# Graph layer on one core: h transposed by DMA in place of TensorE, with attention and aggregation moved within a set

## The chip, the cores and the metric

One NeuronCore of a Trainium2 chip runs the whole program. The metric is device time in microseconds (us); the time of the kernel before is the median of three runs.

## The reference, cut to what matters

There are 128 graphs of 64 nodes with 384 features. With the drawn data every edge has some type, and type 0 means no edge; the layer is

```
h = relu(layernorm(x))                                   # 128 x 64 x 384
hi_t = h @ W1[:384] + dep_emb @ W1[384:] + b1            # per pair i, j
hj_t = h @ W2[:384] + dep_emb @ W2[384:] + b2
relevance = sum(hi_t * hj_t, -1);  A = softmax(where(adj, relevance, -1e9))
out = x + relu((A @ h) @ gcn_w + gcn_b) @ Wo + bo
```

The adjacency holds only 0 and 1 here, so the edge embedding is one vector, and relevance reduces to (h M + bias) h^T plus a row term, with M = W1 W2^T. The aggregation is done on hg = h @ gcn_w.

## The kernel before, in words

The 128 graphs are worked in 16 sets of 512 tokens (NSUP = 16; s counts them). A set is 4 tiles of 128 tokens (KT), each of 2 graphs (GT), and the 384 features are 3 chunks of 128 (DC). The matrix products are split: each float32 operand is a float16 high part and a float16 low part (what the high part leaves), and a product is three float16 matmuls, high by high, high by low and low by high (split_product, L974 to L976).

Five instruction streams, one for each engine, are written out by hand in order, with semaphores between them. A stream is in order: a waiting instruction holds all that stands behind it. In iteration s:

* **TensorE** (PE): G of set s = M^T h^T in three chunks (g_chunk); the transposes of attention of set s-1 (L1137) after the first chunk; the aggregation of set s-1 (L1184, L1189) into three z banks; four tiles of hg of set s (hg_tile); the scores of set s (L1031); 12 transposes of h of set s+1 (L1020, float32, into PSUM); four output tiles of set s-1.
* **ScalarE** (ACT): copies of G (L454), of transposed attention (L532), of z (L545) and of the high part of hg (L459); of the scores (L564); the high part of h^T out of PSUM (L450); the exponentials (L572); and at the end `normalise(s + 2)`, four activations that write h_tok (L441).
* **VectorE** (DVE): high part of G (L706), attention high (L824), high part of z (L829), statistics of set s+2 (L595), row term and low part of hg (L865, L632), masks and scores (L883 to L896), low part of h^T (L601), softmax (L917 to L929), the outputs added into x (L836).
* **GpSimd** (POOL): low part of G (L354), low part of z (L401), the 20 small steps of layer norm's coefficients of set s+2 (L318), then the output bias added to x of set s (L408).
* **SyncE** (SP) issues DMAs: load of set s+4 (L236), four SBUF to SBUF moves of hg (L250, L251), store of a finished set (L241).

So the coefficients of set s+2 need its statistics, `normalise(s + 2)` needs the coefficients, and the h^T of set s+2 is needed by G one iteration later. Ahead of the loop a startup makes M, finds the scales of the weights, and looks whether any edge type over 1 is there (`typed`, skipped here). In the startup PE multiplies hg of set 0 first and then G of set 0. Iterations 1, 14 and 15 and the tail are written out apart.

The eight PSUM banks are shared: `G_BANK = (1, 2, 0)`, `Z_BANK = (3, 4, 5)`, `HG_BANK = (1, 2, 0, 3)`, `T_BANK = (4, 5, 0)` and `O_BANK = (1, 2, 3, 4)`; bank 6 is for scores, bank 7 for attention.

Of the kernel before, what the change touches and what calls it, by code (L numbers as in the profile page):

```python
# [5 lines left out]
def gnn_layer_program(nc, x, adj, emb, W1, b1, W2, b2, gcn_w, gcn_b, Wo, bo, out):  # L6
# [50 lines left out]
    with ctx:  # L57
# [3 lines left out]
        def sem(name):  # L61
# [4 lines left out]
        w1_dep = sb("w1_dep", [DE + 1, D])  # L66
        w2_dep = sb("w2_dep", [DE + 1, D])
        e_col = sb("e_col", [DE + 1, 1])
        e_wide = sb("e_wide", [DE + 1, P])
        q_row = sb("q_row", [P, D])  # L70
        product = sb("product", [P, D])
# [3 lines left out]
        wo_raw = sb("wo_raw", [P, DC, D])  # L75
# [38 lines left out]
        m_raw = x_all[:, NSUP - 5, 0:DC, :]  # L114
        stats6 = sb("stats6", [P, KT, 6])
# [10 lines left out]
        hT_hi = sb("hT_hi", [P, DC, N], f16)  # L126
        hT_lo = sb("hT_lo", [P, DC, N], f16)
# [49 lines left out]
        ty_vec = sb("ty_vec", [P, 2, DC, NT])  # L177
        ty_pq = sb("ty_pq", [P, NT])
        ty_value = sb("ty_value", [P, NT])
        ty_row = sb("ty_row", [P, KT, NT])  # L180
# [5 lines left out]
        G_BANK, Z_BANK, HG_BANK, T_BANK, O_BANK = (1, 2, 0), (3, 4, 5), (1, 2, 0, 3), (4, 5, 0), (1, 2, 3, 4)  # L186

        LAST_Z_BANK = (5, 0, 6)
# [11 lines left out]
            top_types top_types_all types_known consts_made bias_made stats_ready coef_ready h_ready t_done  # L200
            t_high t_split g_done g_copied g_high g_split hg_done hg_high hg_split dot_done s_done scored
# [11 lines left out]
         top_types, top_types_all, types_known, consts_made, bias_made, stats_ready, coef_ready, h_ready, t_done,  # L213
         t_high, t_split, g_done, g_copied, g_high, g_split, hg_done, hg_high, hg_split, dot_done, s_done,
# [19 lines left out]
        def _(sp):  # L234
# [7 lines left out]

            def move_hg(s):
# [20 lines left out]
            for s in range(2, 4):  # L264
                sp.wait_ge(x_loaded, 16 * s)
                load_x(s)

# [10 lines left out]
            with sp.Fori(0, NSUP - 4) as s:  # L278

                sp.wait_ge(x_loaded, 16 * (s + 4))  # L280
                load_x(s + 4)
                move_hg(s + 1)
                store_out(s)
            with sp.Fori(NSUP - 4, LAST) as s:
                move_hg(s + 1)
                store_out(s)
# [8 lines left out]
        def _(pool):  # L295
# [45 lines left out]
            def main_coefficients(s):  # L341

                pool.wait_ge(stats_ready, s + 1)

                if not isinstance(s, int) or s >= 1:
                    pool.wait_ge(h_ready, KT * s)
                coefficients(s, stats6, ln_mul, ln_add, coef_ready)
# [46 lines left out]
            def iteration(s, prev=True, cur=True, nxt2=True):  # L394
# [10 lines left out]
                if cur:  # L405

                    pool.wait_ge(h_ready, KT * (s + 1))
# [14 lines left out]
        def _(act):  # L422
# [21 lines left out]
            def transposed_high(s):  # L444

                if not isinstance(s, int) or s >= 1:
                    act.wait_ge(s_done, s)
                for c in range(DC):
                    act.wait_ge(t_done, DC * s + c + 1)
                    nc.scalar.activation(hT_hi[:, c, :], bank[T_BANK[c]][:, :], ACT.Copy).then_inc(t_high, 1)  # L450
# [40 lines left out]
            transposed_high(0)  # L491
# [28 lines left out]
            def iteration(s, prev=True, prev2=True, cur=True, nxt=True, nxt2=True):  # L520
                z_bank = Z_BANK if cur else LAST_Z_BANK
                for c in range(DC):
# [4 lines left out]
                    if c == (0 if prev2 else DC - 1) and prev:  # L527
# [39 lines left out]
                if nxt:  # L567
                    transposed_high(s + 1)
# [19 lines left out]
        def _(dve):  # L588
# [9 lines left out]
            def transposed_low(s):  # L598
                for c in range(DC):
# [64 lines left out]
            magnitude(0, m_raw[:, 0, :], AX.X, m_peaks)  # L664

# [17 lines left out]
            transposed_low(0)  # L683
# [156 lines left out]
            def iteration(s, prev=True, prev2=True, cur=True, nxt=True, nxt2=True):  # L840
                for c in range(DC):
# [5 lines left out]
                    if c == (0 if prev2 else DC - 1) and prev:  # L847
# [10 lines left out]
                if nxt2 and (prev2 or not prev):  # L858
                    statistics(s + 2)
                if cur:  # L860

                    if prev:
                        for k in range(KT):
# [3 lines left out]
                            hg_low_part(s, k)  # L867
                    else:
# [4 lines left out]
                    if prev and not prev2:  # L873
                        statistics(s + 2)
                    if not prev:

                        transposed_low(1)
# [20 lines left out]
                if nxt and prev:  # L898
                    transposed_low(s + 1)

# [62 lines left out]
        def _(pe):  # L963
# [43 lines left out]
            def transposes(s, prev=True, after_g=False):  # L1007
                pe.wait_ge(h_ready, KT * (s + 1))
                for c in range(DC):
                    if prev and c < 2:  # L1010

                        pe.wait_ge(z_copied, DC * (s - 2) + c + 2)
                    if c == 2 and prev:

                        hg_read(KT * (s - 1) + 3)
                    if c == 2 and after_g:

                        pe.wait_ge(g_copied, DC)
                    for k in range(KT):
# [249 lines left out]
```

## Time and profile before

| what | value |
|---|---|
| median of 3 runs | 427.15 us (426.7 to 428.35) |
| profiled execution: time, span | 427.54 us, 425.3 us |
| PE busy | 377.3 us, 89% |
| DVE busy | 321.3 us, 76% |
| POOL busy | 255.9 us, 60% |
| ACT busy | 230.0 us, 54% |
| mean granted TensorE clock | 0.956 |

The profiled execution took 2.24 us more than its span. Busy time of PE counts modelled ends of matmuls that overlap, so it isn't PE at its peak. A line of the profile can be a helper's: L974 to L976 serve G, hg and the outputs alike, L318 all coefficient steps.

### The profile page before, as it was taken

The page shows a single profiled execution, that of the slowest core. Times are in us where ns is not written, and L with a number is a line of the kernel's source. Part 1 is how long each engine was busy: PE and PEld are TensorE (multiplying, and loading weights), DVE is VectorE, ACT ScalarE, POOL GpSimd, SP SyncE. Part 2 cuts the span into 40 slices and gives each one's busy share as a digit, 9 for nine tenths or more (in the row PEclk, how much of TensorE's full clock was granted, in tenths as well). Part 3 has the DMA queues.
Part 4 walks back from the last instruction along what each step waited for, and adds up shares of the span by engine and source line. Part 5 has one row for each costly group of instructions (what it writes and reads, how often), then busy time and mean ns, then how long its engine had stood idle before and what let it go on. Part 6 is the DMA issues. An engine that isn't in the chain of part 4 may idle for free.

```text
span 425.3 us, 10122 instructions
## 1 busy us (share of the span) xinstructions
PE 377.3 (89%) x3260; PEld 237.1 (56%) x3260; DVE 321.3 (76%) x684; ACT 230.0 (54%) x504; POOL 255.9 (60%) x449
## 2 busy tenths in 40 slices
PE   3719486459999999999999999999999999999986
PEld 3314163355757575665656575756565757566654
DVE  1658264386897988888888888888888897968675
ACT  2255524436565647474747475655555564745441
POOL 2413230798858676777768585858586868681811
PEclk9967978869999999999999999999999999999999
DMA  8881050034133343434343434343333331323134
GB/s 254 231 227 44 0 153 0 0 76 141 36 102 101 84 131 74 148 74 148 74 148 74 148 74 148 74 131 78 107 88 109 94 92 41 74 75 104 46 76 150
DMA packets 38756, 42.81 MB, mean 101 GB/s; under 512 B 2210, under 2 KB 38692, under 8 KB 38740
## 3 DMA queue, kind: packets, MB, share of 16 engines
q1 hardware_dynamic: 38032, 41.62, 33.9%
q10 hardware_dynamic: 644, 0.79, 0.6%
q0 software_dynamic: 64, 0.20, 0.2%
q8 instruction: 8, 0.13, 0.1%
q14 instruction: 8, 0.07, 0.0%
HBM read 17.44 MB, written 12.58 MB: 71 GB/s over the span
## 4 chain that ended last, share of the span: by engine, by line
PE 75%; issue 10%; POOL 6%; DVE 5%; DMA 2%; ACT 1%; POOLq 0%; DVEq 0%; SPq 0%
PE bank L974 20%; PE bank L975 19%; PE bank L976 19%; PE bank L1031 5%; PE bank L1020 4%; PE bank L1189 3%; PE bank L1184 3%; DMA x_all<-in_x_dram 2%; POOL root_sq L318 2%; PE bank L1137 1%; POOL root L318 1%; DVE stats L595 1%; POOL adj_all L379 1%; POOL g_parts L354 1%; POOL var_d L318 1%
## 5 line engine op out<-in xcount | busy, mean ns | idle before, releaser
L354 POOL TENSOR_TENSOR g_parts<-g,g_parts 128x512 f16<-128x512 f32 x45 | 52.0, 1158 | 68.4 <-DVE g_parts L706 68.4
L974 PE MATMUL bank<-gw_hi,hT_hi 128*128 128x385 f16 (+2 forms) x204 | 65.8, 327 | 15.6 <-DVE hT_lo L601 8.0
L454 ACT ACTIVATE g<-bank,pair_bias 128x512 f32<-128x512 f32 x48 | 32.7, 686 | 62.5 <-PE bank L976 62.4
L401 POOL TENSOR_TENSOR z_lo<-z,z_hi 128x512 f16<-128x512 f32 x46 | 56.5, 1253 | 15.2 <-DVE z_hi L829 15.2
L975 PE MATMUL bank<-gw_lo,hT_hi 128*128 128x385 f16 (+2 forms) x204 | 65.3, 325 | 0.1
L976 PE MATMUL bank<-gw_hi,hT_lo 128*128 128x385 f16 (+2 forms) x204 | 65.3, 325 | 0.0
L459 ACT ACTIVATE hg_hi<-bank 128x384 f16<-128x384 f32 x64 | 31.2, 491 | 52.0 <-PE bank L976 52.0
L974 PE MATMUL bank<-wo_hi,z_hi 128*128 128x384 f16 x180 | 58.7, 326 | 0.0
L975 PE MATMUL bank<-wo_lo,z_hi 128*128 128x384 f16 x180 | 58.7, 326 | 0.0
L976 PE MATMUL bank<-wo_hi,z_lo 128*128 128x384 f16 x180 | 58.7, 326 | 0.0
L974 PE MATMUL bank<-hT_hi,m_hi 128*128 128x512 f16 x144 | 54.7, 380 | 1.2 <-DVE hT_lo L601 1.2
L408 POOL TENSOR_TENSOR x_all<-x_all,bo_all 128x1536 f32 (+1 forms) x16 | 55.2, 3447 | 0.1
L975 PE MATMUL bank<-hT_lo,m_hi 128*128 128x512 f16 x144 | 54.6, 379 | 0.0
L976 PE MATMUL bank<-hT_hi,m_lo 128*128 128x512 f16 x144 | 54.6, 379 | 0.0
L829 DVE CAST z_hi<-z 128x512 f16<-128x512 f32 x48 | 45.4, 992 | 4.6 <-ACT z L545 3.7
L441 ACT ACTIVATE h_tok<-x_all,ln_add,ln_mul 128x384 f32 (+1 forms) x64 | 39.8, 693 | 9.0 <-POOL ln_add L318 9.0
L706 DVE CAST g_parts<-g 128x512 f16<-128x512 f32 x48 | 20.3, 427 | 28.6 <-ACT g L454 28.5
L564 ACT ACTIVATE score_parts<-bank 64x256 f32<-64x256 f32 x64 | 24.3, 379 | 27.6 <-PE bank L1031 26.4
L836 DVE SCALAR_TENSOR_TENSOR x_all<-bank,out_scale,x_all 128x384 f32 (+1 forms) x64 | 36.3, 609 | 2.0 <-PE bank L1235 1.9
L974 PEld LDWEIGHTS bank<-gw_hi,hT_hi 128*128 128x128 f16 x204 | 20.1, 100 | 29.2 <-DVE gw_lo L625 8.3
L632 DVE SCALAR_TENSOR_TENSOR hg_lo<-bank,hg_hi 128x384 f16<-128x384 f32 x64 | 34.8, 543 | 1.8 <-ACT hg_hi L459 1.8
L1031 PE MATMUL bank<-hT_hi,g_parts 128*128 128x64 f16 x384 | 26.8, 199 | 9.8 <-POOL g_parts L354 9.8
(128 smaller groups left out, 814.0 us busy)
## 6 DMA issues: line engine op xcount, KB each, us to landing
x_all<-in_x_dram SPq DMA_DIRECT2D x16, 768.0 KB, 5.4
out_dram<-x_all SPq DMA_DIRECT2D x15, 768.0 KB, 3.9
hg_parts<-hg_lo SPq DMA_DIRECT2D x32, 192.0 KB, 3.4
hg_parts<-hg_hi SPq DMA_DIRECT2D x32, 192.0 KB, 3.9
out_dram<-x_all SPq DMA_DIRECT2D x4, 192.0 KB, 1.9
x_all<-in_L_gnn_W_w_dram SPq DMA_DIRECT2D x1, 576.0 KB, 5.6
x_all<-in_L_gnn_W_w_dram ACTq DMA_DIRECT2D x1, 576.0 KB, 6.1
gcn_raw<-in_L_gnn_gcn_w_dram SPq DMA_DIRECT2D x1, 576.0 KB, 11.1
```

What stands on the lines that cost most here:

```text
L354: nc.gpsimd.tensor_tensor(g_parts[:, c, :, 1, :], g_graphs[:, c, :, :], g_parts[:, c, :, 0, :], ALU.subtract).then_inc(g_split, 1)
L401: nc.gpsimd.tensor_tensor(z_lo[:, c, :], z32[:, c, :], z_hi[:, c, :], ALU.subtract).then_inc(z_split, 1)
L408: nc.gpsimd.tensor_tensor(x_all[:, s, :, :], x_all[:, s, :, :], bo_all[:, :, :].broadcast_to([P, KT, D]), ALU.add).then_inc(x_biased, 1)
L441: nc.scalar.activation(h_tok[:, k, :], x_all[:, s, k, :], ACT.Relu, bias=ln_add[:, k:k + 1], scale=ln_mul[:, k:k + 1]).then_inc(h_ready, 1)
L454: nc.scalar.activation(g32[:, c, :], bank[G_BANK[c]][:, :], ACT.Identity, bias=pair_bias[:, c:c + 1], scale=PROJ).then_inc(g_copied, 1)
L632: nc.vector.scalar_tensor_tensor(hg_lo[:, k, :], bank[HG_BANK[k]][:, 0:D], PROJ, hg_hi[:, k, :], ALU.mult, ALU.subtract).then_inc(hg_split, 1)
L829: nc.vector.tensor_copy(z_hi[:, c, :], z32[:, c, :]).then_inc(z_high, 1)
L836: nc.vector.scalar_tensor_tensor(x_all[:, s, k, :], bank[O_BANK[k]][:, 0:D], out_scale[:, 0:1], x_all[:, s, k, :], ALU.mult, ALU.add).then ...
L974: nc.tensor.matmul(dst, lh, rh, start=(c == 0), stop=False)
L975: nc.tensor.matmul(dst, lh, rl, start=False, stop=False)
L976: last = nc.tensor.matmul(dst, ll, rh, start=False, stop=(c == DC - 1))
L1031: last = nc.tensor.matmul(score_bank[:, k, g, :], g_parts[:, d, GT * k + g, :, :], part[:, d, cols], start=(d == 0 and n == 0), stop=(d == ...
```

## The change

h is no longer transposed on PE. ACT writes h twice, as float32 (h_tok) and as its float16 high part (into h_parts); DVE subtracts them in one operation of 128x1536 (`token_low`) to get the low part beside it; and one DMA transpose issued by SP turns the 128x3072 float16 of h_parts into one of two buffers hT[0], hT[1], from which PE reads both parts. In each iteration `token_low(s+1)` stands first on DVE, and ACT waits with `normalise(s)` for the landing of the transpose of set s-1, since h_parts is single. On PE attention's transposes stand behind G's second chunk, the aggregation behind the first hg tile; DVE's statistics of set s+2 stand behind the low part of the first hg tile; the PSUM banks are dealt anew. SP's loop is unrolled, the transpose of set s+2 between load and hg moves. Several startup buffers move into parts of x_all that are free then.

```diff
-        hT_hi = sb("hT_hi", [P, DC, N], f16)
-        hT_lo = sb("hT_lo", [P, DC, N], f16)
+        h_parts = sb("h_parts", [P, KT, 2, D], f16)
+        hT = [sb(f"hT{b}", [P, KT * 2 * DC, P], f16) for b in range(2)]
...
-        G_BANK, Z_BANK, HG_BANK, T_BANK, O_BANK = (1, 2, 0), (3, 4, 5), (1, 2, 0, 3), (4, 5, 0), (1, 2, 3, 4)
+        G_BANK, Z_BANK, HG_BANK, O_BANK = (0, 1, 2), (3, 4, 5), (0, 1, 2, 0), (3, 4, 5, 2)
...
+            def transpose_h(s, half):
+
+                sp.wait_ge(h_split, s + 1)
+                if s >= 2:
+                    sp.wait_ge(s_done, s - 1)
+                sp.dma_start_transpose(hT[half][:, :, :], h_parts[:, :, :, :].rearrange("p k n d -> p (k n d)"))\
+                  .then_inc(hT_landed, 16)
...
             for s in range(2, 4):
                 sp.wait_ge(x_loaded, 16 * s)
                 load_x(s)
+            transpose_h(0, 0)
...
             move_hg(0)
...
+            transpose_h(1, 1)
+            for s in range(LAST):
+                if s + 4 <= LAST:
+                    sp.wait_ge(x_loaded, 16 * (s + 4))
+                    load_x(s + 4)
+                if s + 2 <= LAST:
+                    transpose_h(s + 2, s % 2)
                 move_hg(s + 1)
                 store_out(s)
...
                 if not isinstance(s, int) or s >= 1:
-                    act.wait_ge(t_done, DC * s)
+                    act.wait_ge(h_split, s)
+                    act.wait_ge(hT_landed, 16 * s)
                 for k in range(KT):
-                    nc.scalar.activation(h_tok[:, k, :], x_all[:, s, k, :], ACT.Relu, bias=ln_add[:, k:k + 1],
-                                         scale=ln_mul[:, k:k + 1]).then_inc(h_ready, 1)
...
+                    for to in (h_tok[:, k, :], h_parts[:, k, 0, :]):
+                        nc.scalar.activation(to, x_all[:, s, k, :], ACT.Relu, bias=ln_add[:, k:k + 1],
+                                             scale=ln_mul[:, k:k + 1]).then_inc(h_ready, 1)
...
-            def transposed_low(s):
-                for c in range(DC):
-                    dve.wait_ge(t_high, DC * s + c + 1)
-                    nc.vector.tensor_tensor(hT_lo[:, c, :], bank[T_BANK[c]][:, :], hT_hi[:, c, :],
-                                            ALU.subtract).then_inc(t_split, 1)
+            def token_low(s):
+
+                dve.wait_ge(h_ready, 2 * KT * (s + 1))
+                nc.vector.tensor_tensor(h_parts[:, :, 1, :], h_tok[:, :, :], h_parts[:, :, 0, :],
+                                        ALU.subtract).then_inc(h_split, 1)
...
             def iteration(s, prev=True, prev2=True, cur=True, nxt=True, nxt2=True):
+                if nxt and prev2:
+
+                    token_low(s + 1)
                 for c in range(DC):
...
-                    if c == (0 if prev2 else DC - 1) and prev:
+                    if c == (1 if prev2 else DC - 1) and prev:
                         attention_high(s, prev2)
...
                             hg_low_part(s, k)
+                            if k == 0 and nxt2 and prev2:
+                                statistics(s + 2)
...
             for c in range(DC):
 
-                hg_read(c + 1)
-
-                g_chunk(c, (lambda d: pe.wait_ge(m_split, d + 1)) if c == 0 else None)
+                if c == 0:
+
+                    hg_read(KT)
+                g_chunk(c, 0, (lambda d: pe.wait_ge(m_split, d + 1)) if c == 0 else None)
...
+                for c in range(DC):
+                    if c == 0:
+
+                        hg_read(KT * s)
+                    if c == DC - 1 and prev2:
+
+                        pe.wait_ge(o_added, KT * (s - 1))
+                    g_chunk(c, half, chunk_ready(s) if c == 0 else None)
+                    if c == 1 and prev2:
                         transposed_attention()
+                hg_tile(0)
                 if not prev2:
...
                     transposed_attention()
                     hg_tile(1)
...
+                aggregation()
+                for k in range(1 if prev2 else 2, KT):
+                    hg_tile(k)
```

## Rows read from the trace of the kernel before

**Rows 1.** The chain of work that ended last, of the page

```profile
PE 75%; issue 10%; POOL 6%; DVE 5%; DMA 2%; ACT 1%; POOLq 0%; DVEq 0%; SPq 0%
```

**Rows 2.** Timeline, PE, one set in the loop: start us, us

```profile
203.60 1.51 PE L1020 MATMUL bank<-ident,h_tok 128*128 128x128 f32 x12
204.94 0.33 PE L974 MATMUL bank<-wo_hi,z_hi 128*128 128x384 f16 x1
...
213.08 0.38 PE L1137 MATMUL bank<-ident,att_parts 128*128 128x128 f16 x4 [0.18 <-DVE att_parts L929]
...
225.99 1.51 PE L1020 MATMUL bank<-ident,h_tok 128*128 128x128 f32 x12
```

**Rows 3.** Timeline, POOL, the same set

```profile
201.53 0.21 POOL L318 TENSOR_TENSOR root_sq<-stats 128x4 f32<-128x4 f32 x1
...
208.32 3.45 POOL L408 TENSOR_TENSOR x_all<-x_all,bo_all 128x1536 f32 x1
214.83 1.16 POOL L354 TENSOR_TENSOR g_parts<-g,g_parts 128x512 f16<-128x512 f32 x1 [3.06 <-DVE g_parts L706]
...
220.26 3.69 POOL L401 TENSOR_TENSOR z_lo<-z,z_hi 128x512 f16<-128x512 f32 x3 [0.36 <-DVE z_hi L829]
```

**Rows 4.** Timeline, DVE, the same set, and one stretch of iteration 1

```profile
206.93 1.88 DVE L601 TENSOR_TENSOR hT_lo<-bank,hT_hi 128x512 f16<-128x512 f32 x3
...
209.45 2.60 DVE L919 TENSOR_TENSOR att<-scores,row_inv 128x256 f32<-128x256 f32 x1
...
218.82 3.00 DVE L829 CAST z_hi<-z 128x512 f16<-128x512 f32 x3 [0.15 <-ACT z L545]
...
88.58 4.14 DVE L883 TENSOR_SCALAR masks<-adj_all,row_term 128x64 f32<-128x64 f32 x4
```

**Rows 5.** Timeline, ACT, the same set

```profile
205.41 1.57 ACT L450 ACTIVATE hT_hi<-bank 128x512 f16<-128x512 f32 x3
...
208.77 2.49 ACT L441 ACTIVATE h_tok<-x_all,ln_add,ln_mul 128x384 f32 x4
```

**Rows 6.** Groups by shape: busy us, mean ns, idle before

```profile
L712 DVE TENSOR_TENSOR g_parts<-g,g_parts 128x512 f16<-128x512 f32 x3 | 2.1, 693 | 0.1
L706 DVE CAST g_parts<-g 128x512 f16<-128x512 f32 x48 | 20.3, 427 | 28.6 <-ACT g L454 28.5
L595 DVE BATCH_NORM_STATS2 stats<-x_all 128x6 f32 x48 | 23.1, 540 | 0.0
L632 DVE SCALAR_TENSOR_TENSOR hg_lo<-bank,hg_hi 128x384 f16<-128x384 f32 x64 | 34.8, 543 | 1.8 <-ACT hg_hi L459 1.8
L545 ACT ACTIVATE z<-bank,gcn_bias 128x512 f32<-128x512 f32 x48 | 29.6, 689 | 3.6 <-PE bank L1189 3.6
L459 ACT ACTIVATE hg_hi<-bank 128x384 f16<-128x384 f32 x64 | 31.2, 491 | 52.0 <-PE bank L976 52.0
```

**Rows 7.** DMA queue and issues: packets, MB, share; KB each, us to landing

```profile
q1 hardware_dynamic: 38032, 41.62, 33.9%
...
out_dram<-x_all SPq DMA_DIRECT2D x15, 768.0 KB, 3.9
hg_parts<-hg_lo SPq DMA_DIRECT2D x32, 192.0 KB, 3.4
```

**Rows 8.** Startup: timelines of SP, PE, ACT and POOL

```profile
22.93 6.60 SPq L236 DMA_DIRECT2D x_all<-in_x_dram  x2
...
32.35 0.48 PE L974 MATMUL bank<-gw_hi,hT_hi 128*128 128x384 f16 x1 [8.05 <-DVE hT_lo L601]
...
44.57 0.19 ACT L473 ACTIVATION_READ_ACCUMULATOR z<-adj_all,minus_edge 128x1 f32 x1
...
51.38 0.39 POOL L376 PARTITION_ALL_REDUCE top_all<-top_type  x1 [5.95 <-issue]
```

**Rows 9.** One window of the startup: busy us by engine, clock, DMA share, GB/s

```profile
31.00:33.00 2.00, 0.65 (x3) 0.34 (x4) 2.00 (x5) 1.83 (x4) 0.00 (x0) 0.50 0.94 354
```

**Rows 10.** Waits: engine and line waited for: us, times, longest

```profile
PE bank L1031 <- POOL g_parts L354: 9.8, 1, 9.8
```

More of the change, by code:

```diff
@@ L114, in gnn_layer_program @@
         m_raw = x_all[:, NSUP - 5, 0:DC, :]
+        product, q_row = (x_all[:, NSUP - 4 + n, DC, :] for n in (0, 1))
+        w1_dep, w2_dep = (x_all[0:DE + 1, NSUP - 4 + n, DC, :] for n in (2, 3))
+        wo_raw = x_all[:, NSUP - 10, 0:DC, :]
         stats6 = sb("stats6", [P, KT, 6])
@@ L664, in _ @@
             magnitude(0, m_raw[:, 0, :], AX.X, m_peaks)
+            token_low(0)
             dve.wait_ge(weight_peaks_all, 1)
@@ L857, in iteration @@
                         z_high_part(s - 1, c)
-                if nxt2 and (prev2 or not prev):
+                if nxt2 and not prev:
                     statistics(s + 2)
@@ L1122, in _, with iteration @@
             pe.wait_ge(dot_done, 2 * DC + 1)
-            scores_of(0)
-            transposes(1, prev=False, after_g=True)
-            def iteration(s, prev2=True, cur=True, nxt=True):
+            scores_of(0, 0)
+            def iteration(s, half, prev2=True, cur=True):
                 def transposed_attention():
@@ L1154, in iteration, with aggregation @@
-                for c in range(DC):
-                    if cur:
-                        if c < 2 and prev2:
-                            pe.wait_ge(o_added, KT * (s - 2) + c + 1)
-                        g_chunk(c, chunk_ready(s) if c == 0 else None)
-                    if c == 0 and prev2:
+                def aggregation():
+                    pe.wait_ge(attT_high, GT * s)
+                    pe.wait_ge(attT_copied, s)
+                    hg_read(KT * s)
+                    pe.wait_ge(hg_moved, MOVES * s)
+                    z_bank = Z_BANK if cur else LAST_Z_BANK
+                    for c in range(DC):
+                        if prev2 and cur:
+                            pe.wait_ge(o_added, KT * (s - 2) + c + 1)
+                        if not cur and c == 2:
+                            pe.wait_ge(score_copied, 2 * GT * NSUP)
+                        for k in range(KT):
+                            cols = slice(c * P, (c + 1) * P)
+                            nc.tensor.matmul(bank[z_bank[c]][:, k * P:(k + 1) * P], hg_hi[:, k, cols],
+                                             attT_hi[:, k, :, :], start=True, stop=False)
+                            for g in range(GT):
+                                at = k * P + g * S
+                                last = nc.tensor.matmul(bank[z_bank[c]][:, at:at + S], hg_parts[:, k, g, cols],
+                                                        attT_parts[:, k, g, :], start=False, stop=(g == GT - 1))
+                        last.then_inc(z_done, 1)
@@ L1192, in iteration @@
-                if cur:
-                    for k in range(early, KT):
-                        hg_tile(k)
-                    pe.wait_ge(g_split, DC * (s + 1))
-                    pe.wait_ge(score_copied, 2 * GT * s)
-                    scores_of(s)
-                if nxt:
-                    transposes(s + 1)
-                if not cur:
-                    return
+                aggregation()
+                for k in range(1 if prev2 else 2, KT):
+                    hg_tile(k)
+                pe.wait_ge(g_split, DC * (s + 1))
@@ L1237, in last_output @@
                     last.then_inc(o_done, 1)
[L1239 to L1243 removed]
+            iteration(1, 1, prev2=False)
+            with pe.Fori(1, LAST // 2) as pair:
+                iteration(2 * pair, 0)
+                iteration(2 * pair + 1, 1)
+            iteration(LAST - 1, 0)
+            iteration(LAST, 1)
+            iteration(LAST + 1, 0, cur=False)
             last_output()
```

126 lines of the change are left out of this document (34 added, 92 removed).

## The prediction

> **What bounds the kernel now.** I read the chain that ended last first: PE has 75% of it, so PE looks like the bound [rows 1]. The timeline of PE, from one block of h transposes to the next, gives the loop's period, 225.99 - 203.60 = 22.39 us [rows 2]. Two things in it could go: the transposes, 204.94 - 203.60 = 1.34 us until the next matmul starts, and 0.18 us of waiting ahead of attention's transposes [rows 2]. Without both PE would need 22.39 - 1.34 - 0.18 = 20.87 us a set. But that wait shows that PE isn't alone. POOL starts coefficients at 201.53 and the output bias at 208.32 [rows 3]; the bias holds the softmax product on DVE (2.60 us, ending at 212.05, just after POOL's 211.77) [rows 3, 4]; this releases PE at 213.08, then come aggregation, z, and low z on POOL, 220.26 to 223.95 [rows 2, 3], and the next coefficients, 223.95 - 201.53 = 22.42 us later. So a loop over POOL, DVE, PE and ACT is as long as PE's own work. The change must shorten both.
>
> **How DVE and POOL meet.** The softmax product alone needs little, but beside the bias it ends when POOL's instruction ends. Four masks of iteration 1 take 4.14 us beside back-to-back POOL work [rows 4], one for each POOL instruction; three z casts take 3.00 us where a cast of that size takes 0.43 [rows 4, 6]. I take it that each such DVE operation waits for the end of the POOL instruction that it meets, and then needs about 0.3 us (0.07 for the small attention copies). The old low part of h^T (three in 1.88 us, out of PSUM) was not held so [rows 4].
>
> **The change, part by part, for one set in the loop.** The old loop goes: PE no longer transposes, and the softmax comes before the bias and isn't held by it. What is late next? `normalise(s+2)` still follows the coefficients, but token_low(s+2) stands first on DVE in the next iteration, so everything behind it, G's high parts and attention high, waits for ACT. I follow that loop from the start of the coefficients:
> 1. Coefficients on POOL, 208.32 - 201.53 = 6.79 [rows 3].
> 2. ACT writes h twice: four activations take 2.49, so eight take 2.49 + 4 x 0.60 = 4.89, with 0.08 to start: 4.97 [rows 5]. The 0.60 is their spacing, (2.49 - 0.69)/3.
> 3. token_low, 128x1536, two SBUF sources, float16 out. Nearest row: the same subtraction at 128x512, 693 ns [rows 6]. 1,024 elements more at that row's slope, if 0.16 of it is fixed, give 0.693 + 1.07 = 1.76. The bias (3.45 us from the coefficients' end) is over by then. With 0.03: 1.79.
> 4. G's two high casts, then two attention copies. Both casts are ready at once, so POOL's first low part begins 0.46 after token_low and two of 1.16 follow [rows 3]; each copy is held by one: 0.46 + 2.32 + 0.07 = 2.85.
> 5. Aggregation's first chunk 0.56, ACT's z 0.69 [rows 6], then the z casts: the first held until G's last low part is out, the third until the first low z: the last ends 3.55 after the attention copies.
> 6. Row term and low hg of the first tile 0.65, four statistics at 0.54 but spaced 0.46, 1.9 [rows 6], 0.06 to POOL.
> Sum: 6.79 + 4.97 + 1.79 + 2.85 + 3.55 + 0.65 + 1.9 + 0.06 = 22.56 us, 0.17 more than now. PE then has over 1.5 us of idle time a set, ahead of the aggregation. The removed 1.34 us and ACT's 1.57 us of copies [rows 5] thus buy nothing: they lie beside this loop.
>
> Bounds of the loop: below, activations to float16 at the 0.49 of hg_hi (eight: 3.9, 1.0 less) and token_low at the cast's 0.43 for 512 (1.28, 0.5 less) [rows 6] give 21.1, still over PE's 20.87; above, if the second z cast just misses its gap and is held too, 0.9 more, 23.5.
>
> **The DMA transpose.** No row has one. It moves 128 x 3072 x 2 bytes = 768 KB. Below, it costs what the store of 768 KB does, 3.9 [rows 7]. Above, the hardware queue spent 0.339 x 425.3 x 16 = 2307 us of engines on 38032 packets, 0.061 each [rows 7]; hT's rows of 128 float16 make 3072 pieces, over 16 engines 11.7 us. I take 6, nearer to the store, since the bytes are the same and the pieces smaller. In the loop it can be issued 4.97 + 1.79 = 6.8 us after the coefficients' end, and is needed by the next `normalise` at the next end of coefficients, 22.56 after the first, and by G at about the same time: any landing within some 15 us is hidden, contention with load and store (some 5 us ahead of it on SP) included. If that cover were gone, the period would be the transpose + 6.8 and its issue, some 7.4. SP's hg moves come behind it, issued some 10 us after it, so they aren't held. The second buffer keeps scores out of its way. Bank waits: G's third chunk now waits for all outputs of set s-2, added well before; hg's fourth tile waits for the first tile's low part, which comes just in time. Both at nothing, covered by the idle time ahead of the aggregation. The unrolled SP loop costs nothing: SP waits most of the time.
>
> The Trainium skill, GPSIMD Engine Reference, section Specifications, says that POOL's SBUF interfaces are shared with VectorE, with contention for DVE instructions with two SBUF inputs. Token_low is such an instruction, the PSUM one it replaces was not; the trace agrees for the softmax product. By that rule a quicker normalise would save only up to 1.4 us, as token_low would then meet the bias. This speaks against the change and is within the range above.
>
> **Startup.** Before, the first product waits until 32.35 for h^T [rows 8]. Now SP must first issue the load of set 3, at 22.93 + 6.60 = 29.5 [rows 8], whose packets fill the engines until about 33 (share 0.94 between 31 and 33) [rows 9]. A transpose of 6 us lands between 35.5 (beside) and 39 (behind); I take 37, 4.7 later. G of set 0 then also waits for all four low hg tiles, 0.49 + 0.54 = 1.1 [rows 6]. The last scan of types on ACT ended at 44.76 [rows 8] and follows G's first chunk: now 50.6. POOL was free for it at 45.44 (51.38 - 5.95) [rows 8], so POOL is 5.1 late, and POOL's chain sets the first scores of set 1: PE waits 9.8 us for it [rows 10]. Below: if the 5.95 us of issue can run before the wait is over, 0; above, with 11.7 for the transpose, 10.8. The transpose of set 1 lands some 6 us later than its h^T did; the 9.8 us cover it (gone, it would cost up to 6).
>
> **Head and tail.** Coefficients of set 3 wait for statistics that stand behind token_low of set 2 on DVE: 1.0 late. 12 periods lie between them and the last coefficients: 12 x 0.17 = 2.0. Behind these PE's gain of the last two sets and the longer normalise cancel: 0.
>
> Sum: 427.54 + 5.1 + 1.0 + 2.0 = 435.6. The profiled execution is 0.4 over the median, so I forecast 435.5 for the median, 2% slower.
>
> **Rivals.**
> A. *PE is the bound* (faster). The coefficients' loop is shorter than I think, above all if activations or token_low go at their lower rows, or DVE slips past POOL. For: PE's 75% of the chain; my loop exceeds 22.39 by 0.17 alone. Against: each link has a row, and the rows show DVE held. Full price: 20.87 a set over 14 sets saves 21.3, with startup and head 427.5 - 21.3 + 6.1 = 412. It decides from a loop 0.9 us under mine. Chance 0.22.
> B. *Nothing moves.* Startup hides behind POOL's 5.95 us and the loop stays at 22.4: 427.54 + 1.0, 428. Chance 0.13.
> C. *The DMA is the loop.* At over 15 us each set takes transpose + 7.4. Place: `normalise` and G wait for landing. For: nothing shows its rate; 24 blocks in series at the landing of a small move, 3.4 [rows 7], would be 82, so the price starts at nothing and has no near end. At 20 us: 27.4 x 14 against 22.4 x 14, 70 more, about 500. Against: the piece price gives 11.7. Chance 0.08.
> The Trainium skill, VectorE: DVE Perf Modes, The three transpose paths, gives 1309 ns for a 128x128 block by DMA; 24 in series would be 31 us by estimate, and rival C about 650 us (38.8 a set). No trace here shows it.
> The forecast itself has 0.57.
>
> **The numbers.** About 0.5% (2.1 us) is what a measurement can tell from no change. Faster: A, 0.22. Same: B and a thin edge of the forecast, 0.14. Slower: the rest and C, 0.64. The forecast's own range is 429 (startup hidden, 1.0 + 0) to 452 (loop 23.5 adds 11, transpose at 11.7 adds 5.7). The range reaches into A to 413, which is its full gain; C is left out, and what lies under 413.
>
> **What would show it.** In the profile after: PE's period near 22.6, with idle time ahead of the aggregation, released by attention high on DVE; DVE waiting at token_low for ACT's h; no wait on DVE's softmax for POOL; the transpose landing in 4 to 12 us; the first hg product near 37. It is wrong if the period is under 22, if DVE doesn't wait at token_low, or if PE or ACT wait for the DMA in the loop.

## The result and the profile after

Changed kernel: 442.82 us median (441.54 to 443.47, four runs). Kernel before, beside it: 427.75 us. Ratio 1.035, 95% interval 1.0323 to 1.0377: slower, as forecast, by 15 us where 8 were forecast. The profiled executions differ alike, 440.7 - 425.3 = 15.4 us of span.

Below, a turn is one set's pass through the loop, and an instruction is called held when its row lasts until the instruction of another engine beside it has ended.

The chain that ended last has another look, from the page of the kernel after (compare [rows 1]), with the transpose's own rows of the page:

```profile
DVE 24%; DMA 21%; PE 21%; issue 12%; ACT 11%; POOL 6%; SPq 4%; DVEq 2%; POOLq 0%; ACTq 0%
...
q1 hardware_dynamic: 87696, 54.21, 48.8%
...
hT<-h_parts SPq DMA_TRANSPOSE x16, 8.1
```

PE fell from 75% to 21%, DVE rose from 5% to 24%. The DMA's 21% must be read with care: 19% is `x_all<-in_x_dram`, which in each turn of the loop bridges some 7 us of the chain:

```profile
202.57 6.62 DMA x_all<-in_x_dram
209.18 0.05 issue
209.23 0.06 DVEq L594
```

The chain takes this landing for what released DVE's queue ahead of the statistics. But the load issued at 202.57 is that of set 9, and the statistics that follow (210.64) are of set 8, whose load was issued a turn earlier, at 179.44. They are not released by it, and DVE itself was busy with the z casts until 210.12. A releaser that is inferred from times that lie close together can be an accident, and in a periodic loop the accident repeats. The transpose lands 8.1 us after its issue (median of 16), the queue moves 54 MB where it moved 42 [rows 7].

**Where the 15.4 us arise.** The cleanest clock is the start of one instruction that occurs once a set, the low part of attention on DVE (`SCALAR_TENSOR_TENSOR att_parts<-att,att_parts`):

| | before | after | added |
|---|---|---|---|
| set 0 | 71.24 | 71.79 | 0.55 |
| set 1 | 98.62 | 101.80 | 3.18 |
| set 2 | 122.83 | 130.67 | 7.84 |
| set 13 | 369.18 | 385.22 | 16.04 |
| set 15 | 411.01 | 426.35 | 15.34 |
| end | 425.3 | 440.7 | 15.4 |

Of the 15.4 us, 7.84 come before set 2's attention, 8.20 in the 11 steady turns (23.14 us each against 22.39), and 0.64 goes back after them. The granted clock has no part in the steady turns: it is 1.00 from set 1's attention to set 13's in both kernels.

**A steady turn.** Timeline of DVE after, the set of [rows 4]:

```profile
202.00 1.75 DVE L600 TENSOR_TENSOR h_parts<-h_tok,h_parts 128x1536 f16<-128x1536 f32 x1
203.67 0.76 DVE L705 CAST g_parts<-g 128x512 f16<-128x512 f32 x2
204.34 1.31 DVE L823 COPY attT_hi<-attT_parts 64x256 f16<-64x256 f16 x2
...
219.16 0.42 DVE L921 TENSOR_TENSOR att<-scores,row_inv 128x256 f32<-128x256 f32 x1
219.62 3.58 DVE L928 TENSOR_SCALAR att_parts<-att 128x256 f16<-128x256 f32 x1
223.23 0.42 DVE L931 SCALAR_TENSOR_TENSOR att_parts<-att,att_parts 128x256 f16<-128x256 f32 x1
223.57 1.66 DVE L835 SCALAR_TENSOR_TENSOR x_all<-bank,out_scale,x_all 128x384 f32 x3
225.15 1.75 DVE L600 TENSOR_TENSOR h_parts<-h_tok,h_parts 128x1536 f16<-128x1536 f32 x1
```

and of POOL, ACT and PE after:

```profile
212.82 0.21 POOL L326 TENSOR_TENSOR root_sq<-stats 128x4 f32<-128x4 f32 x1 [0.57 <-DVE stats L594]
...
219.60 3.44 POOL L416 TENSOR_TENSOR x_all<-x_all,bo_all 128x1536 f32 x1
```

```profile
225.29 0.39 PE L976 MATMUL bank<-hT,m_hi 128*128 128x512 f16 x1 [1.18 <-DVE x_all L835]
```

The softmax product ends at 219.58, 0.02 us ahead of the bias add, and escapes it. The next instruction, the high part of attention, starts 0.02 us behind it and needs 3.58 us where it needs 0.29 alone: it ends at 223.20, just behind the bias (223.04). This is so in all twelve steady sets, 2 to 13. In the kernel before, the same bias held the product, for 2.60 us [rows 4]. The residual adds and the low part of h stand behind it. ACT's eight activations (219.93 to 224.82) are over by 225.15, so in a steady turn the low part of h waits for no one, and PE waits for the adds, ahead of G's third chunk.

**The first turn is another loop.** After the coefficients of set 3 (103.90) attention is already done, the bias holds nothing, and DVE after does what was forecast:

```profile
101.80 0.42 DVE L931 SCALAR_TENSOR_TENSOR att_parts<-att,att_parts 128x256 f16<-128x256 f32 x1
...
108.92 1.76 DVE L600 TENSOR_TENSOR h_parts<-h_tok,h_parts 128x1536 f16<-128x1536 f32 x1 [2.98 <-ACT h_parts L451]
110.59 0.76 DVE L705 CAST g_parts<-g 128x512 f16<-128x512 f32 x2
111.26 2.29 DVE L823 COPY attT_hi<-attT_parts 64x256 f16<-64x256 f16 x2
...
115.86 1.70 DVE L828 CAST z_hi<-z 128x512 f16<-128x512 f32 x2
```

and POOL after, from one bias add to the next:

```profile
103.90 3.44 POOL L416 TENSOR_TENSOR x_all<-x_all,bo_all 128x1536 f32<-128x1536 f32 x1
...
120.48 0.21 POOL L326 TENSOR_TENSOR root_sq<-stats 128x4 f32<-128x4 f32 x1 [0.80 <-DVE stats L594]
...
127.04 3.44 POOL L416 TENSOR_TENSOR x_all<-x_all,bo_all 128x1536 f32 x1
```

From bias to bias this turn takes 23.14 us. The same turn of the kernel before takes 118.73 - 99.62 = 19.11. By the rows, ACT's doubled writing and the low part of h put about 2.4 + 1.8 us into it; no run below takes either out of this turn, so that share is read and not tested. Two loops of nearly the same length thus run in the changed kernel: one through ACT's normalising (first turn), one through the bias add that holds attention (steady turns).

### The profile page after: what moved, and what is told of

Read it like the earlier page. It is cut to its first block, busy times and chain, and to the rows that moved or that the text cites. A ratio compares the mean times of both kernels' runs of the same rounds, so it can differ in the third digit from the quotient of the medians.

```text
span 440.7 us, 9440 instructions
## 1 busy us (share of the span) xinstructions
PE 361.1 (82%) x3068; PEld 211.9 (48%) x3068; DVE 341.7 (78%) x652; ACT 243.1 (55%) x520; POOL 260.8 (59%) x449
## 4 chain that ended last, share of the span: by engine, by line
DVE 24%; DMA 21%; PE 21%; issue 12%; ACT 11%; POOL 6%; SPq 4%; DVEq 2%; POOLq 0%; ACTq 0%
DMA x_all<-in_x_dram 19%; DVE att_parts L928 10%; PE bank L976 5%; ACT scores L571 5%; PE bank L978 4%; PE bank L977 4%; PE bank L1016 4%; ACT score_parts L565 4%; DVE x_all L835 3%; DMA hT<-h_parts 2%; DVE hg_lo L631 2%; POOL root_sq L326 1%; SPq L270 1%; DVE att L921 1%; DVE scores L896 1%
## 5 line engine op out<-in xcount | busy, mean ns | idle before, releaser
L976 PE MATMUL bank<-gw_hi,hT 128*128 128x385 f16 (+2 forms) x204 | 65.2, 324 | 25.3 <-DMA hT<-h_parts 19.7
L976 PE MATMUL bank<-hT,m_hi 128*128 128x512 f16 x144 | 55.5, 385 | 26.9 <-DVE x_all L835 13.3
L978 PE MATMUL bank<-gw_hi,hT 128*128 128x385 f16 (+2 forms) x204 | 64.7, 322 | 0.0
L977 PE MATMUL bank<-gw_lo,hT 128*128 128x385 f16 (+2 forms) x204 | 64.5, 321 | 0.0
L976 PE MATMUL bank<-wo_hi,z_hi 128*128 128x384 f16 x180 | 59.7, 331 | 2.2 <-POOL z_lo L409 2.2
L977 PE MATMUL bank<-hT,m_hi 128*128 128x512 f16 x144 | 55.3, 384 | 0.0
L978 PE MATMUL bank<-hT,m_lo 128*128 128x512 f16 x144 | 55.3, 384 | 0.0
L451 ACT ACTIVATE h_tok<-x_all,ln_add,ln_mul 128x384 f32 (+1 forms) x64 | 44.5, 696 | 18.5 <-POOL ln_add L326 18.5
L828 DVE CAST z_hi<-z 128x512 f16<-128x512 f32 x48 | 40.9, 897 | 8.1 <-ACT z L546 7.7
L571 ACT ACTIVATE scores<-scores,exp_bias,exp_scale 128x64 f32<-128x64 f32 x64 | 27.4, 429 | 32.8 <-DVE exp_bias L901 32.8
L928 DVE TENSOR_SCALAR att_parts<-att 128x256 f16<-128x256 f32 x16 | 44.0, 2752 | 0.5
L451 ACT ACTIVATE h_parts<-x_all,ln_add,ln_mul 128x384 f16 (+1 forms) x64 | 44.3, 692 | 0.0
L546 ACT ACTIVATE z<-bank,gcn_bias 128x512 f32<-128x512 f32 x48 | 29.6, 686 | 24.5 <-PE bank L1159 24.5
```

The costliest lines, as they stand in the source:

```text
L451: nc.scalar.activation(to, x_all[:, s, k, :], ACT.Relu, bias=ln_add[:, k:k + 1], scale=ln_mul[:, k:k + 1]).then_inc(h_ready, 1)
L571: nc.scalar.activation(scores[:, k, :], scores[:, k, :], ACT.Exp, bias=exp_bias[:, k:k + 1], scale=exp_scale[:, 0:1], accum_out=row_sum[:, ...
L828: nc.vector.tensor_copy(z_hi[:, c, :], z32[:, c, :]).then_inc(z_high, 1)
L928: nc.vector.tensor_scalar(att_parts[:, :, 0, :], att[:, :, :], A_SCALE, None, ALU.mult).then_inc(att_high, 1)
L976: nc.tensor.matmul(dst, lh, rh, start=(c == 0), stop=False)
L977: nc.tensor.matmul(dst, lh, rl, start=False, stop=False)
```

## The experiments

The texts on record name their theories by letters; H is the hold of attention's high part by the bias add, N the normalising loop, D the DMA queue, and from e5 on T is "two loops, close together". Ratios are to the kernel before, beside each run.

**e1_bias_split** and **e2_before_bias_split**, the bias add in four pieces in either kernel:

```diff
-  nc.gpsimd.tensor_tensor(x_all[:, s, :, :], x_all[:, s, :, :], bo_all[...].broadcast_to([P, KT, D]), ...)
+  for k in range(KT):
+      nc.gpsimd.tensor_tensor(x_all[:, s, k, :], x_all[:, s, k, :], bo_all[:, 0, :], ...)
```

> The changed kernel with POOL's output bias (L416, 128x1536, 3.44 us) cut into four adds of 128x384. Theory H (held): in each set DVE's high part of attention starts beside the bias and is held to its end (3.58 us instead of 0.29), and the adds into x, token_low and G's high parts stand behind it; this makes the 23.15 us period. Then here it is held by the first piece alone (under 1 us), the next bound is my loop over normalise, 22.5 us a set, and the time falls by 0.65 x 13 = 8 to 9, to some 434 us. Theory N (normalise): ACT's eight activations set the period and the hold costs nothing: unchanged, 443 within 2. Theory D (the DMAs' traffic): unchanged too.

> The kernel before with the same cut of the bias (L408). There the softmax product was held for 2.2 us and PE waited 0.18 us a set for it. Theory H: the hold goes, PE alone is left, period from 22.39 to between 22.1 and 22.2, so 3 us less, some 424.5. Theory N or D: unchanged, 427.5 within 1.

Measured: e1 448.9 us, ratio 1.0494 (1.0457 to 1.0531), slower than the changed kernel, against every theory; e2 426.26, 0.998 (0.9962 to 0.9999), 22.26 us a set. DVE of e1:

```profile
222.49 0.89 DVE L921 TENSOR_TENSOR att<-scores,row_inv 128x256 f32<-128x256 f32 x1
223.42 0.98 DVE L928 TENSOR_SCALAR att_parts<-att 128x256 f16<-128x256 f32 x1
224.43 1.11 DVE L931 SCALAR_TENSOR_TENSOR att_parts<-att,att_parts 128x256 f16<-128x256 f32 x1
```

Each of three instructions is now held by one piece, so a third instruction is caught as well, and the pieces take 4.10 us in place of 3.44. The three together take 3.05 us (222.49 to 225.54) where they took 4.49. The shorter hold gains nothing: in ten of the twelve steady sets the low part of h now waits for ACT, up to 1.39 us, and both attention copies are held (2.29 us a pair, 1.31 in the changed kernel). A turn takes 23.51 us on average, close to the 23.36 of e3 below, where the hold is gone altogether. Some 4 us more arise behind set 13; they weren't followed up.

In e2 the gain is about 1 us, between H's 3 and the others' none, so it decides between no two theories: the product still takes 1.11 us and the high part 0.98.

**e3_bias_out**, the bias add on 4 of 384 columns:

> The changed kernel that adds the output bias to the first 4 of 384 columns alone, so that POOL's bias takes 0.2 us instead of 3.44. Theory H: like the cut bias, period 22.5 us, some 434 us; no lower, since normalise's loop doesn't hold the bias. Theory N: unchanged at 443. If the period falls to PE's 20.9 (some 415 us), normalise's loop is not there at all.

Measured 444.53 us, 1.0396 (1.0364 to 1.0427): no gain, as N has it; H alone falls. DVE of e3:

```profile
220.23 0.34 DVE L928 TENSOR_SCALAR att_parts<-att 128x256 f16<-128x256 f32 x1
...
225.46 1.76 DVE L600 TENSOR_TENSOR h_parts<-h_tok,h_parts 128x1536 f16<-128x1536 f32 x1 [2.85 <-ACT h_parts L451]
```

The hold is gone, and in its place the low part of h waits 2.85 us for ACT, in 15 sets (40.6 us in all). A turn takes 23.36 us on average over sets 2 to 13. Here both attention copies are held by a low G (2.28 us a pair, 1.31 in the changed kernel), which makes this loop longer than the one it replaced.

**e4_dma_half_more**, a second DMA transpose of half the size a set, for which `normalise` waits:

> The changed kernel with a second DMA transpose of half the size (128x1536 float16, 384 KB, into a buffer that nobody reads) ahead of each transpose from set 2 on, with normalise waiting for it too. Theory H and N: the transpose is issued 7.3 us after the coefficients' end and needed 16 us later; it lands in 8.1 now and in some 12 here, still hidden: the time within 1.5 us of 443. Theory D: the transpose or its traffic is on the path: some 4 us a set more, 50 or more in all.

Measured 442.27 us, 1.0335 (1.031 to 1.036). The queue moves 59.7 MB in place of 54.2 and nothing changes: from set 2 on the DMA is hidden, D falls.

**e5_low_part_later**:

```diff
-    if nxt and prev2:
-        token_low(s + 1)
     for c in range(DC):
...
         if c == (1 if prev2 else DC - 1) and prev:
             attention_high(s, prev2)
+            if nxt and prev2:
+                token_low(s + 1)
```

> VectorE's low part of h (1.75 us) moves from the start of a set to behind the two copies of the transposed attention, so that no second G cast, copy or aggregation waits for it or for ScalarE's normalising. Two loops (T: in the changed kernel the hold of the attention's high part by the bias add leads, 23.15 us a set; the normalising loop, 23.36 us in e3_bias_out, is close behind it): both have this 1.75 us in them and both lose it, but G's third cast and GpSimd's low G then come 1.75 us later, so GpSimd's coefficients can give some of it back: 22.8 us a set by a schedule of the engines, 12 sets less 0.35 each, 438; at best 23.15 - 1.75 = 21.4 and 422. Rival S (the low part of h is not on the path, the attention's transposes and the third G chunk behind the residual adds are): no change, 442.8.

Measured 450.7 us, 1.0513 (1.0479 to 1.0546), 23.75 us a set; neither. DVE of e5:

```profile
206.00 1.36 DVE L705 CAST g_parts<-g 128x512 f16<-128x512 f32 x1 [0.15 <-ACT g L456]
207.29 1.39 DVE L823 COPY attT_hi<-attT_parts 64x256 f16<-64x256 f16 x2
208.71 1.76 DVE L600 TENSOR_TENSOR h_parts<-h_tok,h_parts 128x1536 f16<-128x1536 f32 x1
210.39 0.42 DVE L705 CAST g_parts<-g 128x512 f16<-128x512 f32 x1
210.72 3.01 DVE L828 CAST z_hi<-z 128x512 f16<-128x512 f32 x3
```

The 1.76 us stay ahead of the z casts and the statistics, since DVE runs one queue. G's third cast comes later, so the last low G meets the z casts and holds them (3.01 us against 2.75), and G's first casts wait for ACT, whose G copies stand behind its normalising. Moving an instruction within a queue that is in the loop doesn't take it out of the loop.

**e6_high_write_out** and **e7_bias_and_high_write_out**, the fp16 write on 4 columns (in e7 the bias add too). The expectation says from set 2 on; the rows show the narrow write 48 times, in sets 4 to 15, so the first turn keeps its whole writes:

```diff
+                    w = D if isinstance(s, int) else 4
-                    for to in (h_tok[:, k, :], h_parts[:, k, 0, :]):
+                    for to, w in ((h_tok[:, k, :], D), (h_parts[:, k, 0, 0:w], w)):
```

> From set 2 on ScalarE's second write (the fp16 high part of h) covers 4 of 384 columns (its values are left out there); ScalarE's normalising falls from 4.8 to about 2.4 us. T (two loops, the bias's hold leads in the changed kernel as it stands): normalising already ends before the adds do (224.82 against 225.15 in the profile), nothing waits for it, so 23.15 us a set and 442 to 443. Rival N (the doubled write is what costs, as the forecast's loop has it): 2.4 us less in each of 12 sets, 414.

> Both at once: bias add on 4 of 384 columns as in e3_bias_out (444.5) and the fp16 high write on 4 of 384 columns. T: each alone gives nothing since the other loop stands right behind it, both together free the set: the normalising loop is 23.36 - 2.4 = 20.96 us and TensorE's own work 21.3 us, so 12 x 1.85 = 22 us less than 442.8: 420. Rival U (a third thing of the change holds the set near 23, e.g. G's third chunk behind all residual adds, the held attention copies, or the new bank order): 440 or more.

Measured: e6 442.82 us, 1.0347 (1.0313 to 1.038), as T has it; N alone falls. e7 428.02, 1.0017 (0.9993 to 1.0042): 14.8 us less than the changed kernel, where T had 22 and U had next to nothing. The four kernels make a square:

| us (us a set) | fp16 write whole | fp16 write narrow |
|---|---|---|
| bias add whole | 442.8 (23.14) | 442.8 (23.14) |
| bias add narrow | 444.5 (23.36) | 428.0 (22.10) |

(e7's 22.10 is each turn from set 3 on; set 2's is 21.03.) Neither edit alone gives anything, both together 15 us: two loops side by side. ACT of e7 tells why it isn't 22:

```profile
215.17 0.71 ACT L452 ACTIVATE h_tok<-x_all,ln_add,ln_mul 128x384 f32 x1 [1.01 <-POOL ln_add L326]
215.78 0.37 ACT L452 ACTIVATE h_parts<-x_all,ln_add,ln_mul 128x4 f16 x1
216.06 0.69 ACT L452 ACTIVATE h_tok<-x_all,ln_add,ln_mul 128x384 f32 x1
```

Four columns still cost 216.06 - 215.78 = 0.28 us, where a whole write is spaced 0.60: four of them save 1.28 us, not 2.4, and 23.36 - 22.10 = 1.26. The normalising loop still binds in e7; DVE waits 1.58 us for ACT at the low part of h.

**e8_low_later_bias_out**, e5 and e3 together:

> The low part of h behind the attention copies (as e5_low_part_later) and the bias add on 4 of 384 columns (as e3_bias_out). T: neither hold nor normalising nor the low part stands ahead of the attention copies; TensorE's own 21.3 us a set is left: 12 x 1.85 less, 420. Rival U (a third thing of the change, see e7): 435 or more.

Measured 448.0 us, 1.0474 (1.044 to 1.0507), 23.69 us a set. Not T, and U only in its number: it is e5's order again. G's first cast waits 3.56 us for ACT's G copy behind normalising, and the low part of h stands ahead of the z casts.

**e9_both_mended**, nothing left out, and **e10_before_bias_after_attention**, the second edit alone, on the kernel before:

```diff
+                for k in range(KT):
+                    dve.wait_ge(h_ready, 2 * KT * s + 2 * (k + 1))
+                    nc.vector.tensor_tensor(h_parts[:, k, 1, :], h_tok[:, k, :], h_parts[:, k, 0, :], ...)
...
+                    pool.wait_ge(att_ready, s + 1)
                     nc.gpsimd.tensor_tensor(x_all[:, s, :, :], x_all[:, s, :, :],
```

> Nothing is left out here: GpSimd starts the bias add of a set only when VectorE has written that set's attention parts (so it can't hold them), and VectorE's low part of h is cut in four tiles, each behind ScalarE's write of that tile. T (two loops close together): the hold is gone as in e3_bias_out (23.36 us a set, the normalising loop), and in that loop only the last tile's low part (0.5 us) is left behind normalising in place of 1.75 us: 22.1 us a set, 12 to 13 sets x 1.05 less than 442.8: 429. Rival V (the bias add, moved later, now holds the low part's tiles or the G casts and copies instead): 440 or more.

> The kernel before with the one edit that the bias add waits for the attention's parts. The hold of 2.2 us on the softmax product (rows 4) goes; e2_before_bias_split took 1.5 us off the time by cutting the add. T: in the kernel before, TensorE's work (20.9 us of 22.39) and the coefficients' loop bind about equally, the hold is worth some tenths a set: 424. Rival V (the later add holds the G casts and the copies and delays low G): 430.

Measured: e9 440.03 us, 1.0266 (1.0226 to 1.0305), 22.66 us a set: V's number, if only just, and V's mechanism. DVE of e9:

```profile
219.54 0.29 DVE L930 TENSOR_SCALAR att_parts<-att 128x256 f16<-128x256 f32 x1
...
221.79 4.03 DVE L602 TENSOR_TENSOR h_parts<-h_tok,h_parts 128x384 f16<-128x384 f32 x4
```

Attention isn't held. The later bias add (220.55 to 224.00) holds the first tile of the low part instead, and the four end at 225.82, 1.1 us behind ACT's last write. The turn is 0.48 us shorter, 5.3 us over eleven, but the wait costs some of it at the end: from set 13's attention to the end this kernel takes 59.7 us, the changed kernel 55.5. What each of the two edits does alone on the changed kernel was not run.

e10 took 424.52 us, 0.9909 (0.9879 to 0.9939): faster than both kernels, and what T forecast. DVE and POOL of e10:

```profile
207.65 0.42 DVE L920 TENSOR_TENSOR att<-scores,row_inv 128x256 f32<-128x256 f32 x1
208.11 0.29 DVE L927 TENSOR_SCALAR att_parts<-att 128x256 f16<-128x256 f32 x1
```

```profile
209.12 3.44 POOL L409 TENSOR_TENSOR x_all<-x_all,bo_all 128x1536 f32 x1 [2.61 <-DVE att_parts L930]
```

POOL waits 2.61 us and a turn falls from 22.39 to 21.92: the delayed add (209.12 to 212.56) meets the residual adds, which read PSUM and take the 1.66 us for three that they take alone, and one G cast, 0.98 us in place of 0.43. Here too the wait costs at the end. Set 13's attention comes 7.3 us earlier, the end only 2.9. In the last two sets of the kernel before, the bias add ran over 8 us ahead of attention (380.74 against 389.46); now it stands behind it, and in the last one it holds the attention copies, 2.77 us where they took 0.47:

```profile
405.92 3.42 POOL L409 TENSOR_TENSOR x_all<-x_all,bo_all 128x1536 f32<-128x1536 f32 x1 [8.85 <-DVE att_parts L930]
...
406.90 2.77 DVE L825 COPY attT_hi<-attT_parts 64x256 f16<-64x256 f16 x2 [1.12 <-ACT attT_parts L533]
```

A kernel with the wait in the loop alone was not run.

**e11_order_undone**, the attention's transposes and copies behind G's first chunk again:

```diff
-                    if c == (1 if prev2 else DC - 1) and prev:
+                    if c == (0 if prev2 else DC - 1) and prev:
```

(on ACT and DVE, and the same on PE.)

> The changed kernel with the attention's transposes and copies back behind G's first chunk (TensorE, ScalarE and VectorE), everything else as changed. T (the new order is no cost, it fits the late attention): G's second chunk (1.95 us) now stands behind the transposes, which wait for attention until 223.7 of the profile, so G's third chunk starts 0.8 us later than now; one cast fewer stands ahead of the copies (0.4 to 1.3 us earlier): between 0 and 0.8 us a set, 443 to 452. Rival O (the new order is what costs): 435 or less.

Measured 450.42 us, 1.0516 (1.0475 to 1.0556), within T: PE waits 2.08 us ahead of the transposes, 0.16 in the changed kernel. The new order is no cost; it saves 7.6 us of what the late attention would cost.

**e12_statistics_first_in_set_1**, the two calls swapped:

> The changed kernel with VectorE's statistics ahead of the low part of h in set 1 alone. In the profile this low part (91.92 to 93.74) holds GpSimd's low z (4.90 us against 3.40 before) and delays the statistics, so the coefficients start at 96.94. T: they start at 95.5 and the bias add of set 1 at 102.5 in place of 103.90: the time is 1.4 us less, 441.4. Rival W (h's transposed parts, 1.9 us later, are what set 2 waits for): the same or 2 us more.

Measured 441.49 us, 1.0305 (1.0267 to 1.0342). The number is T's, its mechanism isn't there: the coefficients start at 96.98, not 95.5. DVE and POOL of e12:

```profile
91.96 1.93 DVE L594 BATCH_NORM_STATS2 stats<-x_all 128x6 f32<-128x384 f32 x4
93.80 2.20 DVE L600 TENSOR_TENSOR h_parts<-h_tok,h_parts 128x1536 f16<-128x1536 f32 x1
```

```profile
92.10 2.29 POOL L409 TENSOR_TENSOR z_lo<-z,z_hi 128x512 f16<-128x512 f32 x2
94.33 2.69 POOL L409 TENSOR_TENSOR z_lo<-z,z_hi 128x512 f16<-128x512 f32 x1
...
104.03 3.45 POOL L416 TENSOR_TENSOR x_all<-x_all,bo_all 128x1536 f32<-128x1536 f32 x1
```

Beside the statistics the first two low z run as if alone. The low part of h, now later, starts ahead of the third and holds that one: the three end at 97.02, 4.92 us in all, where in the changed kernel the same operation held the first and the three took 4.90. So the swap moved the hold and didn't remove it, and the bias add starts 0.13 us later, not 1.4 earlier. The interval overlaps the changed kernel's; the difference isn't shown to be one.

## Why the prediction was right or wrong

**The direction holds, and the reason in its main point.** PE's removed work buys nothing because a loop that starts from POOL's coefficients binds. The loop that was priced, over ACT's normalising, binds in the first turn only; the steady turns follow another one. Rival A (PE is the bound) falls with the period; even in e7, with both loops shortened, a turn takes 22.10, over PE's 20.87. Rival B falls with the time. Rival C falls with e4, and the transpose lands in 8.1 us, within 3.9 to 11.7.

**The loop, steps 1 to 6.** The first turn is the loop that the prediction followed, so it can be checked step by step:

| step | forecast | first turn |
|---|---|---|
| 1 coefficients | 6.79 | 127.04 - 120.48 = 6.56 |
| 2 normalise | 4.97 | 108.92 - 103.90 = 5.02 |
| 3, 4 low part, casts, copies | 4.64 | 113.55 - 108.92 = 4.63 |
| 5 aggregation, z, z casts | 3.55 | 117.56 - 113.55 = 4.01 |
| 6 low hg, statistics, to POOL | 2.61 | 120.48 - 117.56 = 2.92 |
| sum | 22.56 | 23.14 |

Steps 5 and 6 were undersized by 0.46 and 0.31 us: step 5 let the first z cast follow the copies too closely (PE starts 0.24 us behind them, ACT's z comes at 114.56, the first cast at 115.28), and step 6 took 0.06 us for the hand-over to POOL, where 0.49 pass between the statistics' end (119.99) and the coefficients' start.

**"The softmax comes before the bias and isn't held by it"** is the step that was wrong in kind. The product isn't held, by 0.02 us, and the very next instruction is, for 3.58 us. I had looked at the one instruction that was held before, and not at the two behind it. The rows to see it were there: the four masks that are held in [rows 4] are of the same kind, TENSOR_SCALAR. In a steady turn the low part of h therefore starts 5.55 us behind the coefficients' end (5.02 in the first turn), the copies escape one hold in return (1.31 us in each steady turn, 2.29 in the first), and the turn is 23.14 all the same. That the two loops come out alike is luck, and so is it that the wrong step cost little in the number. It hid that the change has two loops: taking out one alone gives nothing (e3, e6). The two loops and their near-equal length in steady turns are shown by the square. What the copies' hold is worth by itself no run shows.

**"Bank waits: both at nothing"** was wrong too: PE waits for the adds 12 times, 13.3 us in all, and 14 times, 6.7 us, for low hg. No run took these away, so whether they cost anything is open. And the row that was read as the old low part of h^T not being held [rows 4] can't show it: the third of them had started before the bias did. That operations out of PSUM aren't held shows in e10, by the residual adds.

**Startup, 5.1 forecast.** The first product came at 38.50, near the 37 forecast, and the last scan of types ended at 52.11, later than the 50.6 forecast. But POOL's row after shows the lower bound was right, its issue ran ahead of the wait:

```profile
52.24 0.39 POOL L384 PARTITION_ALL_REDUCE top_all<-top_type  x1 [5.93 <-ACT z L475]
```

Compare [rows 8]: there the 5.95 us were issue, here the 5.93 us are waiting for ACT, and POOL is 0.86 us late, not 5.1. PE also waits 12.38 us for the landing of set 1's transpose, and that is covered, as forecast: in the profile of e12 the low part of h of set 1 takes 1.76 us where it takes 5.03 in the changed kernel's, the attention copies behind it come 5 us earlier (75.63 against 80.62), and the bias add of set 0 starts at 85.39 against 85.35.

**Head, periods and tail.** The forecast counts up to the coefficients of set 3, from there twelve periods to the last coefficients, and the tail behind them. The two rows before, then the two after:

```profile
92.62 0.22 POOL L318 TENSOR_TENSOR root_sq<-stats 128x4 f32<-128x4 f32 x1
358.29 0.21 POOL L318 TENSOR_TENSOR root_sq<-stats 128x4 f32<-128x4 f32 x1
...
96.94 0.20 POOL L326 TENSOR_TENSOR root_sq<-stats 128x4 f32<-128x4 f32 x1
374.80 0.21 POOL L326 TENSOR_TENSOR root_sq<-stats 128x4 f32<-128x4 f32 x1 [0.57 <-DVE stats L594]
```

| term | forecast | measured |
|---|---|---|
| startup and head | 5.1 + 1.0 = 6.1 | 96.94 - 92.62 = 4.32 |
| twelve periods | 2.0 | (374.80 - 358.29) - 4.32 = 16.51 - 4.32 = 12.19 |
| tail | 0 | 15.4 - 16.51 = -1.1 |
| sum | 8.1 | 15.4 |

So the periods are the term that was mis-sized, by 10 us. 3.99 of their 12.19 are the first one: I had taken the old loop as 22.4 us long everywhere, but its first turn has no hold and is 19.11 from bias add to bias add, so what the new loop adds shows in full there. The other eleven add 0.75 each where 0.17 was forecast. Startup and head came out near their size with the wrong terms: the coefficients of set 2 start 1.59 us late and take 1.21 longer, and low z takes 1.50 longer, held by the low part of h. The coefficients of set 3 then wait for low z, not for the statistics.

**Of what would show it**, three signs failed: PE's idle time stands ahead of G's third chunk, not of the aggregation; attention on DVE is held by POOL after all; and DVE waits for ACT at the low part of h in three sets only, 10.2 us, in none of the steady ones. The last was named as a sign that the forecast is wrong, and for the loop of the steady turns it is. The period, 23.14, the landing and the first product came near what was said.

## What to carry to other kernels

When two loops of near-equal length bind, taking work out of one shows nothing: remove one suspect at a time and then both, and read the square. For each instruction on GpSimd that runs long, ask which VectorE instructions can start within it, all of them, not only the one that the trace before shows held; starting the long one some us later, behind the last instruction that it could hold on the path, was worth 4 us in the kernel before (e10), net of 4.4 us that it costs from set 13's attention on. Whether leaving it out in the last sets gives these back was not run. And price a change against the shortest turn of the old loop too (its first), not only against its steady one.

## What the hardware showed that was not expected

- VectorE's `TENSOR_SCALAR`, float32 to float16 in SBUF with one tensor input, is held to the end of GpSimd's instruction as a product of two is (3.58 us against 0.29). The prediction leaned on one half of the rule that it cited, two SBUF inputs; the Trainium skill, Advanced Engine Details and Errata, section VectorE Performance Modes, also says that VectorE instructions in a mode with two read ports and GpSimd's block each other, and lists `tensor_scalar`, copy and cast among those that have such a mode. The rows of `att_parts` and `attT_hi` agree with it.
- It goes both ways: one of GpSimd's low z, begun 0.15 us behind the low part of h, takes 2.68 us in place of 1.17 in the changed kernel, and 2.69 in e12, begun 0.53 us behind it. Beside the statistics (one SBUF input) two take 2.29, as they do alone.
- A DMA transpose of 128 x 3072 float16, SBUF to SBUF, landed in 8.1 us (5.5 to 9.4) and kept SyncE's queue busy for 3.5 to 6.1 us. That is far from the 31 us, an estimate, that the Trainium skill's figure (VectorE: DVE Perf Modes, The three transpose paths, 1309 ns a block) gave for 24 blocks in series.
- An activation of 4 columns costs 0.28 us of ScalarE's time, one of 384 columns 0.60.
